# Edge groups of 1024, 512 and 256 rows in a sorted segment sum: contiguous rows per partition, and fewer transposes and adds

## The reference

```
aggr = segment_sum(edge_attr, dst, 6250)                 # 100000 x 256 -> 6250 x 256
h    = relu(concat([layernorm(x), aggr]) @ W1 + b1)      # 512 -> 256
h    = relu(h @ W2 + b2)
x    = x + h @ W3 + b3
# then: x = x + sliced_attention(layernorm(x)), 8 heads of 64, softmax over 64 slices
```

## Time and profile before

| | us |
|---|---|
| median of 3 runs | 752.93 (752.92 to 753.28) |
| the profiled execution's own time | 754.04 |
| its span (first to last instruction) | 752.2 |
| TensorE busy (matmuls) | 726.1 (97%) |
| VectorE / ScalarE / GpSimd busy | 452.1 / 262.5 / 244.0 |
| HBM read / written, MB | 112.35 / 6.40 |

### The profile page before, as it was taken

How to read it: one execution, slowest core, us unless ns; L and a number is a source line. 1 busy time by engine, 2 the same in 40 slices (tenths; PEclk the granted TensorE clock), 3 DMA queues, 4 the chain that set the end, 5 groups by cost and what they waited for, 6 DMA issues and landing times.

```text
span 752.2 us, 13498 instructions
## 1 busy us (share of the span) xinstructions
PE 726.1 (97%) x3865; PEld 472.6 (63%) x3865; DVE 452.1 (60%) x1158; ACT 262.5 (35%) x460; POOL 244.0 (32%) x306
## 2 busy tenths in 40 slices
PE   6999999999999999699999989999999999899997
PEld 3667777677677776365566655555555555588886
DVE  5667666676676666054444378788887887532222
ACT  4344443444444435111221223333333333233331
POOL 3011011010110111213323336565655556244441
PEclk9999999999999999899999999999999999999999
DMA  8999999999999995210000000000000000012222
GB/s 301 375 369 384 384 385 384 384 385 384 385 384 384 385 384 209 71 44 1 0 0 0 0 1 1 0 0 0 0 0 0 0 0 1 0 43 77 76 70 75
DMA packets 70136, 118.96 MB, mean 158 GB/s; under 512 B 4925, under 2 KB 19608, under 8 KB 70120
## 3 DMA queue, kind: packets, MB, share of 16 engines
q1 hardware_dynamic: 69304, 118.50, 43.9%
q10 hardware_dynamic: 816, 0.26, 0.1%
HBM read 112.35 MB, written 6.40 MB: 158 GB/s over the span
## 4 chain that ended last, share of the span: by engine, by line
PE 94%; DMA 2%; DVE 2%; issue 1%; ACT 0%; SPq 0%; DVEq 0%; ACTq 0%
PE ps L1002 23%; PE ps L1239 11%; PE ps L1155 11%; PE ps L1163 11%; PE ps L1047 6%; PE ps L1080 6%; PE ps L1088 6%; PE ps L1098 6%; PE ps L1014 5%; PE ps L1172 3%; PE ps L1039 2%; PE ps L1147 1%; DMA ring_mem<-edge_attr_in 1%; DMA big<-dst_in 1%; PE ps L969 0%
## 5 line engine op out<-in xcount | busy, mean ns | idle before, releaser
L1002 PE MATMUL ps<-ring_mem,side 128*64 128x256 f32 x1564 | 184.1, 385 | 3.7 <-DMA ring_mem<-edge_attr_in 3.5
L719 DVE TENSOR_TENSOR big<-big,ps 128x128 f32 x391 | 112.5, 288 | 73.4 <-issue 31.3
L1002 PEld LDWEIGHTS ps<-ring_mem,side 128*64 128x64 f32 x1564 | 111.4, 137 | 62.5 <-issue 18.4
L558 ACT ACTIVATE side<-ps 128x512 f32<-128x512 f32 x98 | 58.5, 597 | 145.7 <-PE ps L1002 145.3
L1163 PE MATMUL ps<-side,ring_mem 128*128 128x512 f32 x196 | 92.3, 593 | 1.0 <-ACT ring_mem L591 1.0
L1155 PE MATMUL ps<-ring_mem,xn 128*128 128x512 f32 x196 | 92.3, 593 | 0.6 <-DVE ring_mem L877 0.6
L452 POOL TENSOR_TENSOR var_e<-mv,eps 128x2 f32<-128x2 f32 (+1 forms) x25 | 13.1, 522 | 242.9 <-DVE mv L705 242.9
L653 DVE TENSOR_TENSOR side<-iota_w,rel 128x512 f32<-128x512 f32 x98 | 66.3, 678 | 20.6 <-PE ps L1014 20.5
L1239 PE MATMUL ps<-side,ring_mem 128*128 128x256 f32 x360 | 77.9, 379 | 0.0
L506 POOL TENSOR_TENSOR ring_mem<-ring_mem 128x512 f32<-128x512 f32 x49 | 67.0, 1366 | 30.9 <-DVE ring_mem L877 30.9
L1239 PEld LDWEIGHTS ps<-side,ring_mem 128*128 128x128 f32 x360 | 68.4, 190 | 9.3
(11 more groups left out here) (138 smaller groups left out, 889.2 us busy)
## 6 DMA issues: line engine op xcount, KB each, us to landing
ring_mem<-edge_attr_in SPq DMA_DIRECT2D x97, 1024.0 KB, 9.0
x_sb<-x_in SPq DMA_DIRECT2D x24, 256.0 KB, 7.3
result<-ring_mem SPq DMA_DIRECT2D x24, 256.0 KB, 2.1
ring_mem<-edge_attr_in SPq DMA_DIRECT2D x1, 512.0 KB, 6.1
ring_mem<-L_gnn_W_in SPq DMA_DIRECT2D x2, 256.0 KB, 3.4
xn<-L_ffn_W_x_in SPq DMA_DIRECT2D x1, 512.0 KB, 3.5
ring_mem<-L_ffn_W_fx_in SPq DMA_DIRECT2D x1, 512.0 KB, 4.1
ring_mem<-L_ffn_W_out_in SPq DMA_DIRECT2D x1, 512.0 KB, 5.2
```

The lines of the kernel that those rows point to most:

```text
L558: act.activation(win_sb[:, s % 2, :], ps[:, SUM_BANKS[s % 2], :], ACT.Copy).then_inc(win_ready, 1)
L719: dve.tensor_tensor(win, win, pair[:, :, (g % 2) * WINDOW:(g % 2 + 1) * WINDOW], ALU.add).then_inc(groups_added, 1)
L1002: last = mm(ps[side_of * WINDOW:(side_of + 1) * WINDOW, SUM_BANKS[s % 2], pair * F:(pair + 1) * F], lhsT=hot[0:parts, s, g * ROWS_PER_PART ...
```

## The change

Chunks stay 1024 edges and the ring stays four slots. Inside a chunk the grouping changes with the density of the destinations:

- chunks 0 to 39: one group of 1024 edges, a partition holds 8 consecutive edges, 8 KB in one piece
- chunks 40 to 83: two groups of 512, a partition holds 4 consecutive edges each, two pieces of 4 KB
- chunks 84 to 97: four groups of 256 as before

On TensorE, ScalarE and VectorE both first kinds run the same code, with `groups` = 2. For a whole-chunk group the two halves of its subtiles share one base, which stands twice in the table. A chunk then makes a 128x256 block: one copy of 256 columns instead of 512, two transposes instead of four, two adds instead of four, and 8 registers per four chunks instead of 16. The matmuls of the sums are as many and as large as before. The table is made from rows of 1024 destinations (40 rows, then 44 and 14). The second part of the table is made after chunk 3's turns, no longer after chunk 0's sums, and the `far` flag at chunk 5. The general path is rewritten for the new grouping. The diff, cut to its core:

```
+WHOLE = 40
+PAIRED = 84
+def sums_ahead(c, groups):
+    if isinstance(c, int):
+        return 2 * min(c, PAIRED) + CHUNK_GROUPS * max(0, c - PAIRED)
+    return c * 2 if groups == 2 else c * CHUNK_GROUPS - 2 * PAIRED
+def run_chunks(eng, step, peel_front, last_trip, total, apart=False):
+    for t in range(peel_front * UNROLL):
+        step(t, t % UNROLL, t // UNROLL, 1 if apart else 2)
+    loops = [(peel_front, WHOLE // UNROLL, 1), (WHOLE // UNROLL, PAIRED // UNROLL, 2)]
+    for lo, hi, groups in loops if apart else [(peel_front, PAIRED // UNROLL, 2)]:
+        with eng.Fori(lo, hi) as i:
+            for s in range(UNROLL):
+                step(i * UNROLL + s, s, i, groups)
+    for t in range(PAIRED, PAIRED + UNROLL):
+        step(t, t % UNROLL, t // UNROLL, CHUNK_GROUPS)
+    with eng.Fori(PAIRED // UNROLL + 1, last_trip) as i: ...
 # SyncE
+            def chunk_rows(c, groups):
+                rows = edges[bass.ds(c * CHUNK_EDGES, CHUNK_EDGES), :]
+                return rows.rearrange("(g p k) f -> p g (k f)", g=groups, p=P) if groups > 1 else rows.rearrange(
+                    "(p k) f -> p (k f)", p=P)
-            sp.dma_start(dst_i[:, 0, :], dst[0:tile_edges].rearrange("(p e) -> p e", e=GROUP)).then_inc(dst0_in, 16)
+            sp.dma_start(dst_one[0:WHOLE, :], dst[0:WHOLE * CHUNK_EDGES].rearrange("(c e) -> c e", e=CHUNK_EDGES)
+                         ).then_inc(dst0_in, 16)
-                    sp.dma_start(ring[:, s].rearrange("p g k f -> p g (k f)"),
-                                 edges[bass.ds(c * CHUNK_EDGES, CHUNK_EDGES), :].rearrange(
-                                     "(g p k) f -> p g (k f)", p=P, k=ROWS_PER_PART)).then_inc(edge_in[s], 16)
+                    sp.dma_start(slot(s, groups), chunk_rows(c, groups)).then_inc(edge_in[s], 16)
-            run_steps(sp, chunk, CHUNKS, 1, EDGE_TRIPS - 1)
+            run_chunks(sp, chunk, 1, EDGE_TRIPS, CHUNKS, apart=True)
 # ScalarE
+                cols = groups // 2 * F
-                act.activation(win_sb[:, s % 2, :], ps[:, SUM_BANKS[s % 2], :], ACT.Copy).then_inc(win_ready, 1)
+                act.activation(win_sb[:, s % 2, 0:cols], ps[:, SUM_BANKS[s % 2], 0:cols], ACT.Copy).then_inc(win_ready, 1)
 # VectorE
+            relative(WHOLE, base_one, dst_one, rel_one)
+            dve.wait_ge(prep_t, 1)
+            dve.wait_ge(prep_v, into_table(0, WHOLE, 6))
             for c in range(3):
                 one_hot(c, c)
+            dve.wait_ge(dst_in, 16 * 4)
+            relative(PAIRED - WHOLE, base_two, dst_two, rel_two)
+            relative(FEW, base_few, dst_few, rel_few)
 # in VectorE's chunk
+                if isinstance(c, int) and c == UNROLL:
+                    rest_of_table()
-                for g in range(CHUNK_GROUPS if before(c, FULL_CHUNKS) else TAIL_GROUPS):
-                    dve.wait_ge(groups_added, c * CHUNK_GROUPS + (CREDIT + g))
+                for g in range(groups if before(c, FULL_CHUNKS) else TAIL_GROUPS):
+                    dve.wait_ge(groups_added, sums_ahead(c, groups) + (CREDIT + g))
 ...
 # TensorE, sums and turn
-                for pair in range(CHUNK_PAIRS):
-                    for k in range(ROWS_PER_PART):
+                per = SUBTILES // groups
+                for pair in range(groups // 2):
+                    for k in range(per):
                         for side_of in range(2):
                             g = pair * 2 + side_of
 ...
+                            t = g * per + k
-                                      lhsT=hot[0:parts, s, g * ROWS_PER_PART + k, :], rhs=ring[0:parts, s, g, k, :],
+                                      lhsT=hot[0:parts, s, t, :], rhs=ring8[0:parts, s, t, :],
 ...
-                pe.wait_ge(groups_added, c * CHUNK_GROUPS + (CREDIT - (UNROLL - 1) * CHUNK_GROUPS))
-                for pair in range(CHUNK_PAIRS):
+                behind = sums_ahead(c - 3, groups) if past(c, 3) else -2 * (3 - c)
+                pe.wait_ge(groups_added, behind + CREDIT)
+                for pair in range(groups // 2):
                     for h in range(KF):
 ...
 # TensorE's chunk
-                if isinstance(c, int) and c == 0:
-                    rest_of_table()
+                turn(c - 1, s - 1, groups)
+                turn(c, s, groups)
+                if isinstance(c, int) and c == 3:
+                    rest_of_table()
+                if isinstance(c, int) and c == UNROLL + 1:
+                    far_row()
```

More of the change, by code:

```diff
@@ L46, in before @@
     return not isinstance(t, int) or t < n
+def sums_ahead(c, groups):
[12 more added lines that the diff above has]
+        step(t, t % UNROLL, t // UNROLL, CHUNK_GROUPS)
+    with eng.Fori(PAIRED // UNROLL + 1, last_trip) as i:
+        for s in range(UNROLL):
+            step(i * UNROLL + s, s, i, CHUNK_GROUPS)
+    for t in range(last_trip * UNROLL, total):
+        step(t, t % UNROLL, t // UNROLL, CHUNK_GROUPS)
 def run_steps(eng, step, total, peel_front, loop_trips):
@@ L322, in rest_of_dst @@
                 row = dst.rearrange("(a e) -> a e", a=1)
[L323 to L328, removed]
+                tail = E - FULL_CHUNKS * CHUNK_EDGES
+                sp.dma_start(dst_few[FEW - 1:FEW, 0:tail], row[:, E - tail:E]).then_inc(dst_in, 16)
@@ L329, in chunk @@
+                sp.dma_start(dst_few[FEW - 1:FEW, tail:TAIL_GROUPS * GROUP],
+                             row[:, E - (TAIL_GROUPS * GROUP - tail):E]).then_inc(dst_in, 16)
+            def chunk(c, s, i, groups):
                 if past(c, UNROLL):
@@ L381, in _ @@
+            with sp.If(far > 0):
+                with sp.Fori(0, WHOLE) as c:
+                    reload(c, 1)
+                with sp.Fori(WHOLE, PAIRED) as c:
+                    reload(c, 2)
+                with sp.Fori(PAIRED, FULL_CHUNKS) as c:
+                    reload(c, CHUNK_GROUPS)
+                reload_last()
             sp.wait_ge(edges_done, 2)
@@ L654, in one_hot @@
                                   where.unsqueeze(2).broadcast_to(shape), ALU.is_equal).then_inc(hot_ready, 1)
[L656 to L662, removed]
-                return made
@@ L665, in into_table, with relative @@
-            def into_table(t0, n):
-                for k in range(ROWS_PER_PART):
[L667 to L670, removed]
+            def relative(rows, base, ids, to):
+                n = base.shape[1]
+                of = ids[0:rows, :].rearrange("c (g e) -> c g e", g=n)
+                dve.wait_ge(prep_v, then(dve.tensor_reduce(base, of, AX.X, ALU.min)))
+                dve.wait_ge(prep_v, then(dve.tensor_scalar(base, base, 0.0, float(N), ALU.max, ALU.min)))
+                for g in range(n):
+                    made = then(dve.tensor_scalar(to[0:rows, :].rearrange("c (g e) -> c g e", g=n)[:, g, :], of[:, g, :],
+                                                  base[:, g:g + 1], None, ALU.subtract))
+                return made
@@ L689, in _ @@
[L689 to L693, removed]
+            bases_one = then(dve.tensor_copy(base_i[0:1, 0:2 * WHOLE].rearrange("a (c g) -> a c g", g=2),
+                                             ps[0:1, 7, 0:WHOLE].unsqueeze(2).broadcast_to([1, WHOLE, 2])))
@@ new lines, in _, with far_chunk @@
+                PER_CHUNK = 3 + 2 * WIDES
+                def far_chunk(c, steps):
+                    ahead = c * PER_CHUNK + 8
+                    dve.wait_ge(gen_d_in, c * 16 + (16 if len(steps[1]) == UNROLL else 32))
+                    dve.tensor_copy(g_abs, g_dst).then_inc(gen_v, 1)
+                    dve.tensor_scalar(g_cov, rel[:, bass.ds(c, 1), :].rearrange("p c t -> p (c t)"),
+                                      float(WINDOW), float(4 * AGG), ALU.is_lt, ALU.mult).then_inc(gen_v, 1)
+                    dve.wait_ge(gen_v, ahead + 2)
+                    dve.tensor_tensor(g_abs, g_abs, g_cov, ALU.add).then_inc(gen_v, 1)
+                    for half_of, tiles in enumerate(steps):
+                        for w in range(WIDES):
+                            turn = half_of * WIDES + w
+                            dve.wait_ge(gen_v, ahead + (3 + turn))
+                            dve.tensor_scalar(g_win, g_abs, float(w * WIDE), None, ALU.subtract).then_inc(gen_v, 1)
+                            dve.wait_ge(gen_v, ahead + (4 + turn))
+                            for t in tiles:
+                                dve.tensor_scalar(g_hot[:, t % UNROLL, :], g_iota, g_win[:, t:t + 1], None,
+                                                  ALU.is_equal).then_inc(gen_hot, 1)
+                            dve.wait_ge(gen_sums, c * (2 * WIDES) + (turn + 1))
+                            view = agg[:, :, w * WIDE:(w + 1) * WIDE]
+                            last = dve.tensor_tensor(view, view, ps[:, 0:2, 0:WIDE], ALU.add)
+                            last.then_inc(groups_added, 1)
+                            dve.wait_ge(groups_added, c * (2 * WIDES) + (CREDIT + ALL_SUMS + turn + 1))
@@ new lines, in base_row @@
+            def base_row(rows, base, bank, col):
```

(8 more changed lines are left out.)

233 lines of the change are left out of this document (121 added, 112 removed).

## The result

| | before | after |
|---|---|---|
| median, us (runs) | 753.11 (4; 752.92 to 754.10) | 742.05 (4; 739.92 to 742.60) |
| profiled execution, us | 754.04 | 739.92 |
| its span | 752.2 | 738.1 |

The ratio is 0.9842, with a 95% interval of 0.9829 to 0.9855. The forecast was 742.8, in 736.5 to 749.5. The profiled execution is the fastest of its kernel, and that of the kernel before lies 0.9 us above its median. So the traces show 14.1 us of gain where the medians show 11.1.

A forecast was written before the change was run, and what follows sets the result against it. The prediction took the edge stage as bound by its load, with TensorE alone behind it. From the profiled 754.04 us, -10.5 for packets and +0.4 for code gave 743.9, or 742.8 in medians, range 736.5 to 749.5.

The forecast's parts named there:

- The bound: Edge stage: the load sets the trip of four chunks at 11.60 us, TensorE alone would need about 11.48.
- Transposes, adds, copies: Edge stage: 18.3 us of TensorE transposes and 48 us of VectorE adds go, copies shorten; worth 0 alone.
- The packet term: Edge loads of chunks 0 to 83: 1664 fewer packets per DMA engine save 10.5 us.
- f: Fixed part of a DMA packet's time in the edge loads, taken as 6.3 ns; each ns worth 1.66 us.
- outer bound of 10.9: Edge loads: upper limit of the fixed packet cost in ns, from a stretch at 408 GB/s; would save 18.1 us.
- 2 x 45.6 - 84.9: Edge loads: twice the 1 KB packet's ns less the 2 KB packet's, giving 6.3 ns for a zero-length packet.
- f of 1 ns: Edge loads: low end of a rival with 1 to 4 ns fixed per packet, 746.5 to 751.4 us; chance 0.09.
- The 0.4 us predicted for code: Edge stage: one or two more instruction fetches on the DMA engines cost 0 to 2 us, taken as 0.4.
- The start: First table and chunk 0: table 1.6 us later, chunk 1's sums earlier; taken as 0, from -1.5 to +1.5 us.
- The byte limit: Edge loads, rival: 386 GB/s whatever the packet, so 752.9 us plus or minus 1.5; chance 0.12.
- Slower large packets: Edge loads, rival: 8 KB packets slower per byte, 19 us more over 84 chunks, near 772; chance 0.07.
- TensorE's floor: Edge stage, rival: trips fall to TensorE's 10.61 us, time 733 to 738; chance 0.12.

The follow-up runs named there:

- `work_alone`: The changed kernel's new grouping, with halved transposes and adds, but 2 KB loads kept: 754.84 us against 753.66 for the kernel before, ratio 1.0015.
- `packets_alone`: The changed kernel's 8, 4 and 2 KB loads, but every chunk summed as four groups as in the kernel before: 757.16 us, ratio 1.0059.
- `half_sums`: The changed kernel with half of the subtiles left out of the sums of chunks 0 to 83: 740.25 us (two runs).
- `four_kb`: The changed kernel with 4 KB pieces in chunks 0 to 39 too, groups of 1024 kept: 743.25 us, ratio 0.9858.
- `x_split`: The changed kernel with the load of the last 106 rows of x cut into 96 and 10: 741.65 us against 741.46 for the control.

## Why the prediction was right

**The bound.** It said that the stage waits for the load, with TensorE 1% below, read from a landing and not from the busy shares. `work_alone` (11.60 us a trip with 0.87 less work) and `packets_alone` (11.48, the predicted floor) show both sides of it.

**Transposes, adds, copies at nothing by themselves.** Right: `work_alone` is 0.15% slower than before.

**The packet term was mis-sized.** Predicted: f = 6.3 ns, 10.5 us in all, trips of 10.96 and 11.19 (by its own f the first should read 11.00). Measured: 9.1 to 9.5 ns, trips of 10.70 and 10.99, so 21 clean trips would bring 10 x 0.90 + 11 x 0.61 = 15.7 us. That is outside the 4 to 8.5 ns given as the forecast's own range, and inside the outer bound of 10.9. The step that failed is 2 x 45.6 - 84.9. Both numbers came from a rate printed as 386. Without rounding on the way it gives f = 6.9. With 387 GB/s it gives 10.6, and with 385 3.1. One GB/s is 3.7 ns, and the text gave it less room than that. Two more slips change nothing: the flat rate fills 12 slices of the earlier trace rows and not 13, and f of 1 ns gives 751.7 us and not 751.4.

**What gave it back.** Odd trips, which the prediction did not have, take 0.2 to 1.2 us each. From chunk 7 to chunk 83 clean trips would bring 8 x 0.90 + 11 x 0.61 = 13.9 us, and the three profiles have 11.8, 11.3 and 10.9 of them. The second and the third lose another 0.4 and 0.8 us in chunks 84 to 95. The 0.4 us predicted for code has no counterpart: the 12.05 us trip is a longer turn. The two trips up to chunk 7 bring 1.0 to 1.4 us, where clean ones would have brought 1.8. With what differs behind the edge stage this turns 15.7 into 11.5 to 14.1. So the time was hit more closely than its terms, and that is luck: the packet term was 5 us too small, and the odd trips were missing.

**The start.** Predicted: 0, with chunk 0 near 9.5. It began at 8.57, as the subtraction of 1024 elements took 0.75 us and not 1.15:

```profile
3.96 1.21 DVE L718 TENSOR_REDUCE base_col<-big 40x1 f32<-40x1024 int32 x1 [3.81 <-DMA big<-dst_in]
5.39 0.75 DVE L721 TENSOR_SCALAR big<-big,base_col 40x1024 f32<-40x1024 int32 x1
```

The 1.6 us won up to chunk 8 is a little less than what eight to nine chunks of 8 KB would bring (0.22 each). So the start itself is near 0, but no run takes it alone.

**The rivals.** The byte limit is out: 2 KB and 8 KB move at 384 and 409 GB/s with TensorE out of the way in both. Slower large packets are out: 8 KB is the fastest size. TensorE's floor was nearer than thought: 10.61 against trips of 10.70, so with 8 KB the expected idle time of TensorE did not come. The Trainium skill gives 512 B for line rate (DMA: Bandwidth & Descriptors, Specifications). This does not hold here, where 4 KB and 8 KB are each faster than the size below. The 3.5 ns that the prediction estimated from the Trainium skill's 3 cycles per packet (DMA: Bandwidth & Descriptors, Why small descriptors are slow) is a third of the 9.1 to 9.5 measured.

**What stays open.** The cause of the odd trips. They are rare in `half_sums`, where TensorE is far below the load, and in the two profiles with the split load (none and one before chunk 84), and they are absent from the steady part of the kernel before. One reading is that some engines have run ahead of the slowest ones and find no issued load, since a slot comes free only when TensorE, now 1% below the load, has finished with it. Against it, `four_kb` has such a trip although TensorE is 0.4 us a trip below the load. The kernel before has a microsecond with a share of 0.65 (41 to 42 us) and loses nothing by it. And in chunks 84 to 95, where loads and sums are as before, the second and third profile have trips of 12.1 and 12.4 us. Single profiles are no proof, and the median of `x_split` did not move.

## What to carry to other kernels

When a stage has two engines within 1% of each other, a change to either alone reads as worthless or worse. Ask for the floor of each, and change both. A full DMA queue and a busy TensorE do not say which of them waits: compare when a load lands with when its first reader starts. A price that is the difference of two rates needs more digits than a page prints. Take it from whole trips, or keep its full rounding error in the range.

## What the runs showed of the hardware

A load in pieces of 2, 4 and 8 KB takes 11.60, 10.99 and 10.70 us a trip, which is about 9.3 ns per packet beside its bytes. Short idle spells of the DMA engines appear in a stage whose queue is else full (a share of 0.67 in one microsecond), and their cause is open. The 106 rows of the last tile of `x` in one load, instead of 96 and 10, cost the kernel before 0.8 us. The spread of one kernel's times differs from set to set: 2.7 to 4.2 us for the changed kernel, 0.9 for `four_kb`, and 1.3, 2.1 and 3.4 for the kernel before in three sets. A loop that nobody touched took 0.37 us more per trip in one of the kernels, 3.6 us in all, which is more than some of the effects under study. Differences between kernels are safer read from the stage that was changed than from the total. And a trip is safer read from the chunk that waits to the next one that waits: from another chunk, work of another engine that changes between the two is counted in.
